# Two result-free 128x512 products in each of the first two passes of the odd head pairs of the first attention

## What is computed

```python
qkv = einsum('bsh,hf->bsf', x, w_qkv) + b_qkv          # 768 columns
q, k = rotary(q), rotary(k)                            # first 4 of 16 columns
scores = where(causal, einsum('bhqd,bhkd->bhqk', q, k), -inf)
probs = softmax(scores); attn = einsum('bhqk,bhkd->bhqd', probs, v)
x = layernorm(x + attn @ w_out + b_out)
# then: gated feed-forward, linear attention, six feed-forward blocks
```

## Time and profile before

| | |
|---|---|
| runs shown | 1239.93, 1243.96, 1245.25 us, median 1243.96 us |
| profiled execution | 1239.62 us, its span 1237.7 us |
| TensorE busy | 1068.4 us, 86% of the span |
| first attention's passes | from 54.5 to about 326 us |

### The profile page before, as it was taken

The page is one execution under the profiler, slowest core; times in us unless marked ns, Lnnn a source line. Parts: engine busy times, 40 slices in busy tenths (PEclk is TensorE's granted clock), DMA queues, the critical chain, the costliest instruction groups (busy, mean ns, idle before and its releaser), DMA issues. The chain is left out here.

```text
span 1237.7 us, 20729 instructions
## 1 busy us (share of the span) xinstructions
PE 1068.4 (86%) x6653; PEld 876.2 (71%) x6653; DVE 773.8 (63%) x2190; ACT 619.8 (50%) x1181; POOL 300.8 (24%) x425
## 2 busy tenths in 40 slices
PE   4888898899756688827878999999999999999995
PEld 3545554555345578816766998899899899899895
DVE  1456676767364277883477566765775775775664
ACT  2255666565313744435326545655654664664650
POOL 2334344452202120110012021231242232232200
PEclk9879999998787889858998999999999999999998
DMA  4000000000063000000012100110100100100111
GB/s 164 18 1 19 2 19 19 18 1 19 1 221 120 1 1 0 0 0 3 1 35 69 35 35 1 35 35 0 34 34 0 34 27 7 34 8 26 35 35 34
DMA packets 28588, 36.56 MB, mean 30 GB/s; under 512 B 1412, under 2 KB 25704, under 8 KB 28520
## 3 DMA queue, kind: packets, MB, share of 16 engines
q1 hardware_dynamic: 25912, 31.80, 7.6%
q10 hardware_dynamic: 2608, 3.93, 0.9%
HBM read 31.40 MB, written 4.19 MB: 29 GB/s over the span
## 5 line engine op out<-in xcount | busy, mean ns | idle before, releaser
L1863 ACT ACTIVATE G<-ps,bias_col 128x512 f32<-128x512 f32 x192 | 134.9, 703 | 188.9 <-PE ps L1781 177.4
L1796 PE MATMUL ps<-w_h,G_h 128*128 128x256 f32 x768 | 217.7, 283 | 1.4 <-DVE rsum L1924 1.4
L1796 PE MATMUL ps<-w_h,G_l 128*128 128x256 f32 x768 | 217.3, 283 | 0.0
L1796 PE MATMUL ps<-w_l,G_h 128*128 128x256 f32 x768 | 217.1, 283 | 0.0
L1915 DVE TENSOR_TENSOR G_l<-G,G_h 128x512 fp32r<-128x512 f32 x192 | 135.8, 717 | 63.8 <-ACT G_h L1864 63.7
L1743 POOL TENSOR_TENSOR x_a<-xn,mlp_g 128x1024 f32<-128x1024 f32 x20 | 72.5, 3628 | 367.7 <-DVE xn L1947 367.7
L1019 DVE CUSTOM_DVE_ANT_0 ps<-ps,q_mask 128x128 f32<-128x128 f32 (+3 forms) x256 | 121.6, 512 | 62.2 <-PE ps L866 58.1
L1781 PE MATMUL ps<-xT_h,w_h 128*128 128x512 f32 x384 | 154.1, 401 | 1.7 <-PEq L1396 1.7
L812 ACT ACTIVATE probs<-ps 128x512 f32<-128x512 f32 (+3 forms) x256 | 98.2, 437 | 113.0 <-PE ps L877 112.3
L1781 PE MATMUL ps<-xT_h,w_l 128*128 128x512 f32 x384 | 152.6, 397 | 0.0
L1781 PE MATMUL ps<-xT_l,w_h 128*128 128x512 f32 x384 | 152.6, 397 | 0.0
(11 more groups left out here) (248 smaller groups left out, 2138.5 us busy)
## 6 DMA issues: line engine op xcount, KB each, us to landing
w_raw<-L_ffn_W_T SPq DMA_DIRECT2D x12, 1024.0 KB, 5.0
hs<-L_attn_hidden_states SPq DMA_DIRECT2D x8, 512.0 KB, 3.5
x_kept<-hs SPq DMA_DIRECT2D x4, 512.0 KB, 2.9
w_raw<-x_kept SPq DMA_DIRECT2D x2, 1024.0 KB, 5.7
out<-xn SPq DMA_DIRECT2D x4, 512.0 KB, 2.9
w_raw<-L_ffn_ent_w_T SPq DMA_DIRECT2D x1, 1024.0 KB, 10.2
w_raw<-L_ffn_ent_pw SPq DMA_DIRECT2D x1, 1024.0 KB, 12.3
qT<-neg_rows SPq DMA_DIRECT2D x64, 2.0 KB
```

Of the source, the lines that this page charges most:

```text
L1796: mm = pe.matmul(ps[:, 4 + t // 2, (t % 2) * D:(t % 2 + 1) * D], x[:, b % 2, f, t * P:(t + 1) * P], w[:, f, :], start=(k == 0), stop=(k == ...
L1863: act.activation(G32[:, n % 4, :], ps[:, n % 4, :], ACT.Gelu, bias=bias)
```

## The change

After `score_pass` in r = 0 and r = 1 of every odd pair TensorE now does two products of 512 columns with the identity (`ident_r`) as weights and 512 columns of the first layer's projection weights (`wqkv_h`) as moving operand, with start and stop set, into the outputs bank. Nobody reads the results: the first `value_pass` of the group, in r = 2, starts the bank anew. There are 4 odd pairs x 2 passes x 4 entries = 32 such passes, 64 products and 64 weight loads. A wait stands ahead of them, on the same count of `a_out` on which the `value_pass` of the group waits in r = 2.

```diff
+            def keep_streaming(i, p):
+
+                pe.wait_ge(s["a_out"], i * GROUPS + p // 2 + 1)
+                for c in range(KC):
+                    pe.matmul(outputs, ident_r[:, :], wqkv_h[:, c, 0:S], start=True, stop=True)
+
             def max_rows(i, when, p, pair):
 
                 pe.wait_ge(s["v_neg"], pair + 3)
...
                         score_pass(i, p, r)
+                        if p % 2 and r < 2:
+                            keep_streaming(i, p)
 
                         if p % 2 and r >= 2:
                             value_pass(i, p // 2, r - 2)
```

## The result

The changed kernel took 1255.81 us in the median of five runs (1247.83 to 1257.48), the kernel before 1243.96 us (1239.93 to 1245.25): a ratio of 1.0082, 95% interval 1.0055 to 1.0109, or 10.2 us at 1243.96 (the medians themselves lie 11.9 us apart). Both are slower; the two intervals meet at 1.0055 to 1.0061, some 7 us. 1255.8 us is within the stated range by 0.2 us; the forecast point was 1246.

A forecast was written before the change was run, and what follows sets the result against it. TensorE was taken to set the pace in the first attention. 1239.62 + 10.2 net cost (15.7 gross less 5.5 hidden) - 8.2 clock gain = 1241.6 us, carried over to the median 1246; range 1235 to 1256.

The forecast's parts named there:

- The bound: First attention: TensorE sets the pace, so added products lengthen the run unless they fill waits or speed something else.
- The price: Odd pairs, r = 0 and 1: two 512-column products cost 0.467 us a pass at the higher clock, 14.9 us in all.
- The wait: Ahead of the new products: the added wait for the copy of the outputs costs nothing.
- What is hidden: Behind the new products: TensorE waits for x_l, neg_rows and others hide 5.5 us of the 15.7 us gross cost.
- Products at the lower clock: Passes (1, 0) and (1, 1) of entry 0, in the slow start, add 0.8 us to the cost.
- What it gives back: First attention: falls of TensorE's clock prevented, 27 us at 0.30 us for each us, 8.2 us gained.
- the 34 us: Lower-clock time in seven stretches of the first attention, of which four fifths were forecast to go.
- the first rival: First attention: the clock doesn't answer, the products cost the full 10.2 us, around 1254 us; chance 0.30.
- theory C: Four products a pass, 0.86 us, keep the clock: half-clock time from 51 to under 20 us, ratio under 1.014.
- the case that I held likeliest: First attention: gain by the clock and cost nearly equal, between 1238 and 1250 us, chance 0.50.
- The third rival: Stages from 326 to 680 us: shifted start changes their clock, up to 3 us either way; no chance of its own.
- The second rival: First attention: the clock stays up throughout, -5.5 to -10 us, around 1236 us; chance 0.20.

The follow-up runs named there:

- e1: Changed kernel with only the wait on the copy of the outputs, its 64 products left out: ratio 1.0002 to the kernel before.
- e12: The changed kernel itself, unaltered, measured again in twelve further runs: ratio 1.0042 to the kernel before, 5.2 us slower.
- e4: Changed kernel with four products instead of two in each of the 32 passes: ratio 1.0136 to the kernel before.
- e11: Changed kernel with products only in r = 1 of pair 1 and r = 0 of pair 5, 8 passes: ratio 1.0029 to the kernel before.
- e9: Changed kernel with products only in r = 0 of pair 1 and r = 1 of pair 5, 8 passes: ratio 0.9966 to the kernel before.
- e5: Changed kernel with products in r = 3 of even and r = 0 of odd pairs, one pass earlier, 32 passes: ratio 1.0006 to the kernel before.
- e13: As e9, with four products in each of the 8 passes: ratio 0.9963 to the kernel before.
- e2: Changed kernel with products only in pairs 1 and 5, 16 passes: ratio 1.0045 to the kernel before.

## Why the prediction was half right

**The bound.** Right: TensorE sets the pace, 64.53 of 70.80 us busy in entry 1 before and 68.47 of 73.90 after, and a product without a wait behind it lengthened its pass by what it takes (the next lines).

**The price.** 0.467 us for a pass: measured 0.37 to 0.47 in the undisturbed passes of pairs 3 and 7 of entries 1 and 2. Right.

**The wait.** Free, as argued: e1, 1.0002.

**What is hidden.** Right for x_l (1.12 to 0.46 us, the pass no longer than before). For neg_rows the waits shrank to nothing in entries 0 and 2 and from 0.51 to 0.29 us in entry 1, so they hid 0.2 to 0.5 us. The net cost of 10.2 us can be checked with the trace: the passes grew by 13.8 us, of which 13.1 us more half clock at 0.22 are 2.9, leaving 10.9; in e12 10.4 - 0.6 = 9.8. For e4 the same working gives 20.8 + 0.9 = 21.7 against the 23.9 added up, for e11 6.5 - 2.9 = 3.6 against 3.3, for e9 -4.2 + 3.1 = -1.1 against 0.8. In these the cost side held within about 2 us. It did not in e5, 3.6 by this working where over 10 were expected, nor quite in e13, 0.8 against 3.9: both times more was hidden than I had counted.

**Products at the lower clock.** Wrong in size: "passes (1, 0) and (1, 1) of entry 0 lie in the slow start, which adds 0.8". 25 and 21 products (e12) lay there, not four, at some 0.2 us more each: about 4 us that the sum lacks. The passes do not show them; TensorE's idle time in them fell from 28.2 to 21.2 us (269.5 - 241.3 and 283.3 - 262.1), so that more than the 5.5 us of the sum may have been hidden. Which waits made up for it isn't shown.

**What it gives back.** This is the step that failed: "I take four fifths of the 34 us". Four fifths were 27 us at 0.30, 8.2 us of time. Measured were 14 ± 4 us (e12), in the first five runs none that shows, at 0.12 to 0.22: 0 to 3 us. With 10.2 us of cost the sum should have been +7 to +10, and 5.2 and 10.2 were found. The mechanism that I gave half of the chance is there, sized three times too large or more. The 0.43 us of the first rival and of theory C in e4 (0.86 for four products) is an estimate, half of the 0.85 us of a pass at the lower clock; at the higher clock the 384-column products came every 0.18 us, not at half of 0.32, and a pass's two products at 0.467 by the earlier trace rows. The traced execution bears every sign that I had named for the first rival (the clock doesn't answer, 1254 us): clocks as before, and an end of the passes at 337 us, where it said 336. That 1255.8 us lies inside the range, by 0.2 us, is owed to the room made for that rival and to luck, not to the case that I held likeliest, whose own range ended at 1250. Only e12, at 5.2 us, lies between the two.

Why so little came back stays open. I read a fall of the clock as belonging to the passes just behind which it began, and the new products went there. In the changed kernel's trace five of the eight falls between the slow start and the end of the passes begin ahead of the odd pair's first product, in entry 1 at 172.3 us, with that product at 173.22; the other three begin in the products. Passes without a value pass begin earlier, with r = 2 and 3 of the even pair before. That the products stand one pass too late is a guess from this, and the means do not bear it out: one pass earlier (e5) the half-clock time is 20 ± 5 us below the kernel before, in the changed kernel's passes (e12) 14 ± 4, and e9, whose eight passes are all among the changed kernel's, has 18 ± 4 less. In r = 1 of pair 1 and r = 0 of pair 5 (e11) nothing measurable goes. One more thing stays open: e2 has the passes of e9 and those of e11 and came out at 203 us, e9 at 182. Why the added passes undo what the others bring no run shows.

**The third rival.** The stages behind took 3.3 us more in the trace, nearly all of it right behind the passes (31.5 us where it was 28.2, with a clock of 0.57 against 0.68). It may be part of the spread between executions, as foreseen without a sign, but that isn't shown: from the last score pass to the first output product of the feed-forward blocks (L1804, L1796 before) the two traces without products take 360.2 and 360.0 us (before, e1), the twelve with products 360.2 to 367.5, eleven of them over 362. Products in the first attention may thus lengthen, through the clock, stages that they don't touch; two traces are too few to tell.

**The second rival** fell for this kernel; for e9 and e13 it holds in direction, at 4 to 5 us.

## What to carry to other kernels

Work without a result cost its full price here wherever TensorE set the pace (0.37 to 0.47 us a pass in pairs 3 and 7, where 0.467 had been added up), and nothing ahead of a wait that doesn't depend on it (pair 1, r = 0, of entry 1: 3.54 us where it was 3.55): look for such waits and put it there and nowhere else, as in e9. Whether it keeps TensorE's clock up, and where it would have to stand for that, can't be read from the fall that it is to prevent; it has to be judged by the mean clock of many runs, since one trace of the same work differed from another by 17 us at the lower level. A fall was worth less than the duration of its products suggests, here 0.12 to 0.22 us for each us and not 0.45; that part of the work in it waits for others anyway is my guess at the reason, which no run isolates.

## What the runs showed of the hardware

The granted clock of one and the same program varied from run to run: half-clock time over the span has a standard deviation of 13 us about 203 us over 29 runs of the kernel before, whose times have one of 3.4 us. More passes with products did not mean a better clock: 16 passes in pairs 3 and 7 went with 212 ± 4 us at the lower level, 8 passes in two places with 182 ± 4 (203 and 200 before). And dense or nearly empty weights made no difference to it that these runs can tell (193 ± 6 and 189 ± 3 us, with 200 and 203 before).
